# A gated recurrence: k normalised in channels by rows like q, two products on ScalarE, single buffers

## The reference, cut to what matters

```python
q = silu(causal_dwconv(xn @ Wq, qconv_w, qconv_b))      # 4 taps
k = silu(causal_dwconv(xn @ Wk, kconv_w, kconv_b))
v = xn @ Wv
beta = sigmoid(xn @ Wb + bb)                            # one per token and head
q = layernorm(q per head, qn_w, qn_b); k = layernorm(k per head, kn_w, kn_b)
def step(S, inp):                                       # over the tokens
    S = (1.0 - b) * S + b * (v_t[..., :, None] * k_t[..., None, :])
    o_t = einsum('bhvk,bhk->bhv', S, q_t)
o = o * silu(xn @ Wg); s = o @ Wo
```

## Time and profile before

| engine | busy us | share of the span |
|---|---|---|
| TensorE (PE) | 2504.8 | 95% |
| VectorE (DVE) | 1813.8 | 69% |
| ScalarE (ACT) | 1083.8 | 41% |
| GpSimd (POOL) | 848.1 | 32% |

### The profile page before, as it was taken

One profiled execution on the slowest core, in us unless ns is written; L12 is line 12 of the kernel. 1 busy time (PEld: TensorE's weight loads), 2 busy tenths in 40 slices (PEclk: granted clock), 3 DMA queues, 4 the chain that ended last, 5 costly groups with the idle time before them and its releaser, 6 DMA issues. The chain is left out here.

```text
span 2627.0 us, 43782 instructions
## 1 busy us (share of the span) xinstructions
PE 2504.8 (95%) x15296; PEld 2215.4 (84%) x15296; DVE 1813.8 (69%) x3332; ACT 1083.8 (41%) x1513; POOL 848.1 (32%) x442
## 2 busy tenths in 40 slices
PE   4889999999999999999999999997899998999997
PEld 4778888889999989999989999996788887888886
DVE  5589999988988888889888989887421222433232
ACT  5454455444545444444444444443433323322221
POOL 1245545434343434343434343444100000211220
PEclk8989999999999999999999999998999999999998
DMA  7555555654445464444465444543561101431320
GB/s 272 171 177 170 192 186 176 211 192 161 160 153 168 160 224 160 165 163 152 160 215 179 155 162 158 171 154 105 164 224 49 64 32 64 135 138 49 112 87 25
DMA packets 232134, 395.10 MB, mean 150 GB/s; under 512 B 58358, under 2 KB 159990, under 8 KB 219130
## 3 DMA queue, kind: packets, MB, share of 16 engines
q1 hardware_dynamic: 125946, 192.21, 22.4%
q10 hardware_dynamic: 97408, 176.71, 19.9%
q0 software_dynamic: 8704, 25.19, 3.1%
HBM read 304.88 MB, written 97.55 MB: 153 GB/s over the span
## 5 line engine op out<-in xcount | busy, mean ns | idle before, releaser
L1005 DVE SCALAR_TENSOR_TENSOR xn_rows<-ps_proj,conv,xn_rows 128x1021 f32<-128x1021 f32 x381 | 486.6, 1277 | 11.6 <-ACT xn_rows L895 2.5
L1208 PE MATMUL ps_proj<-xt_hi,w_hi 128*128 128x512 f32 x1008 | 413.0, 410 | 14.5 <-DVE xn_rows L1005 8.1
L1210 PE MATMUL ps_proj<-xt_hi,w_lo 128*128 128x512 f32 x1008 | 397.9, 395 | 0.0
L1209 PE MATMUL ps_proj<-xt_lo,w_hi 128*128 128x512 f32 x1008 | 396.6, 393 | 0.0
L786 POOL TENSOR_TENSOR rc_k_state<-rc_tok_k,k_norm_rows 128x1024 f32<-128x1024 f32 x64 | 153.7, 2402 | 587.4 <-DVE rc_q_silu L1052 502.6
L1230 PE MATMUL ps_proj<-wv_hi,xt_hi 128*128 128x256 f32 x1024 | 294.9, 288 | 0.6 <-PEq L75 0.6
L1231 PE MATMUL ps_proj<-wv_lo,xt_hi 128*128 128x256 f32 x1024 | 289.5, 283 | 0.0
L1232 PE MATMUL ps_proj<-wv_hi,xt_lo 128*128 128x256 f32 x1024 | 289.4, 283 | 0.0
L1208 PEld LDWEIGHTS ps_proj<-xt_hi,w_hi 128*128 128x128 f32 x1008 | 191.1, 190 | 53.5 <-issue 11.7
L819 POOL TENSOR_TENSOR rc_rstd_shift<-rc_small,rc_minus_half 128x16 f32<-128x16 f32 x64 | 187.2, 2924 | 124.8 <-DVE rc_small L1036 124.8
L1210 PEld LDWEIGHTS ps_proj<-xt_hi,w_lo 128*128 128x128 f32 x1008 | 190.3, 189 | 42.7
(11 more groups left out here) (181 smaller groups left out, 5766.8 us busy)
## 6 DMA issues: line engine op xcount, KB each, us to landing
rc_q_rows<-scratch_q_rows ACTq DMA_DIRECT2D x64, 1024.0 KB, 4.9
rc_decay_all<-scratch_decay ACTq DMA_DIRECT2D x64, 512.0 KB, 3.7
rc_cum_all<-scratch_cum ACTq DMA_DIRECT2D x64, 512.0 KB, 3.9
scratch_o<-rc_o_sb ACTq DMA_DIRECT2D x64, 512.0 KB, 4.4
w_hi<-scratch_w_split SPq DMA_DIRECT2D x48, 512.0 KB, 4.1
w_lo<-scratch_w_split SPq DMA_DIRECT2D x48, 512.0 KB, 5.2
wv_hi<-scratch_wv_split SPq DMA_DIRECT2D x24, 512.0 KB, 3.9
wv_lo<-scratch_wv_split SPq DMA_DIRECT2D x24, 512.0 KB, 4.8
```

The costliest lines, as they stand in the source:

```text
L1005: nc.vector.scalar_tensor_tensor(out=act_cm[j][:, back:], in0=projected[:, 0:L - back], scalar=conv[par][:, j, t:t + 1], in1=act_cm[j][:, ...
L1208: nc.tensor.matmul(out, hi, xt_hi[:, k, cols], start=k == 0, stop=False)
L1209: nc.tensor.matmul(out, hi, xt_lo[:, k, cols], start=False, stop=False)
L1210: last = nc.tensor.matmul(out, lo, xt_hi[:, k, cols], start=False, stop=k == KC - 1)
```

## The change

For k the turn back to channels goes away. The rows of k's 1/sigma and shift are turned, stored and loaded like q's (32 rows instead of 16 in one store; two loads), VectorE scales k in channels (`k_silu` has two buffers and `k_rows` is new), and ScalarE applies weight and bias one step later, for D. The product of v and beta becomes eight ScalarE operations of 128 columns behind the silu of q, and the decay of k's state eight ScalarE operations behind the tap of k. `decay_all`, `cum_all`, `k_cm` and `o_sb` have one buffer instead of two, with waits for the head before instead of the one before that. The loads of the sums move behind the decayed state in ScalarE's list. In the first stage one semaphore takes the place of two. The buffers of `ps_work` are now chosen by the parity of the step too.

```diff
-        k_cm = two("k_cm", [P, L])
+        k_cm = sb("k_cm", [P, L])
-        decay_all = two("decay_all", [P, L])
-        cum_all = two("cum_all", [P, L])
+        decay_all = sb("decay_all", [P, L])
+        cum_all = sb("cum_all", [P, L])
-        o_sb = two("o_sb", [P, NC, P])
+        o_sb = sb("o_sb", [P, NC, P])
...
             def load_decay(par, i, pair):
-                after_step(act, "dmat_done", i - 2)
+                after_step(act, "dmat_done", i - 1)
...
             def load_cum(par, i, pair):
-                after_step(act, "states_done", i - 2, NC - 1)
-                after_step(act, "q_cum_done", i - 2)
+                after_step(act, "states_done", i - 1, NC - 1)
+                after_step(act, "q_cum_done", i - 1)
...
+                def ready_k():
+                    after_step(act, "k_scaled", D_.i, 2)
+                    after_step(act, "scores_mm", D_.i - 1)
+                    nc.scalar.activation(k_cm[:], k_silu[D_.par][:], ACT.Identity,
+                                         bias=norm[:, 1, 1:2], scale=norm[:, 1, 0:1]).then_inc(S["k_ready"], 1)
...
+                def load_rows(j, X):
+                    after_step(act, "rows_stored", X.i, 16)
+                    after_step(act, "qk"[j] + "_scaled", X.i - 1, 2)
+                    parts = row(scratch["rows"], X.i)[2 * L * j:2 * L * (j + 1)]
+                    act.dma_start((q_rows, k_rows)[j][:].rearrange("p k t -> p (k t)"), parts.partition_broadcast(P)
+                                  ).then_inc(S["qk"[j] + "_rows_loaded"], 16)
+
+                def decayed_state():
+                    after_step(act, "k_tokens_done", C_.i)
+                    after_step(act, "dmat_done", C_.i)
+                    for c in range(NC):
+                        last = nc.scalar.activation(k_state[C_.par][:, c], k_state[C_.par][:, c], ACT.Copy,
+                                                    scale=dmat[C_.par][:, c, P - 1:P])
+                    last.then_inc(S["k_state_done"], 1)
...
+                def gate_values():
+                    after_step(act, "v_projected", B_.i)
+                    after_step(act, "outputs_mm", 2 * B_.pair - 3)
+                    stand(act, keep["carrier_sp"])
+                    first = B_.par * VC
+                    for c in range(VC):
+                        for h in range(2):
+                            columns = slice((2 * c + h) * P, (2 * c + h + 1) * P)
+                            last = nc.scalar.activation(
+                                v_beta[B_.pair_par][:, first + c, h], ps_proj[:, B_.par, columns], ACT.Identity,
+                                scale=keep["beta_steps"][:, first + c, bass.ds(B_.pair * 2 + h, 1)])
+                    last.then_inc(S["v_beta_done"], 1)
...
                 if B_.live:
                     silu(0)
+                    gate_values()
+                if D_.live:
+                    ready_k()
+                if B_.live:
                     silu(1)
...
                 if C_.live:
-                    ready(0, "q_scaled", 2, q_silu[C_.par][:], "q_ready", q_cm[C_.par])
+                    ready_q()
+                    load_rows(1, C_)
...
-                if C_.live:
-                    ready(1, "k_back", 1, work(KB), "k_ready", k_cm[C_.par])
-                    load_cum(C_.par, C_.i, C_.pair)
                 if B_.live:
                     tokens()
                 if A_.live:
                     tap(1)
+                if C_.live:
+                    decayed_state()
+                    load_cum(C_.par, C_.i, C_.pair)
                 if B_.live:
                     store_rows()
...
-                    load_rows()
+                    load_rows(0, B_)
...
 # VectorE
+            def scale(j, C_):
+                n = "qk"[j]
+                values, rows = (q_silu, k_silu)[j][C_.par], (q_rows, k_rows)[j]
+                after_step(dve, n + "_rows_loaded", C_.i, 16)
+                after_step(dve, n + "_turned", C_.i)
+                nc.vector.tensor_tensor(values[:], values[:], rows[:, 0], ALU.mult).then_inc(S[n + "_scaled"], 1)
+                after_step(dve, n + "_scaled", C_.i, 2, 1)
+                nc.vector.tensor_tensor(values[:], values[:], rows[:, 1], ALU.add).then_inc(S[n + "_scaled"], 1)
...
-                if B_.live:
-                    gate_values()
                 if C_.live:
...
-                    scale_q()
+                    scale(0, C_)
...
                 if C_.live:
-                    after_step(dve, "k_tokens_done", C_.i)
-                    after_step(dve, "dmat_done", C_.i)
-                    nc.vector.tensor_tensor(k_state[C_.par][:], k_state[C_.par][:],
-                                            dmat[C_.par][:, :, P - 1:P].to_broadcast([P, NC, P]), ALU.mult
-                                            ).then_inc(S["k_state_done"], 1)
+                    scale(1, C_)
...
 # TensorE
-                if C_.live:
-                    after_step(pe, "k_normed", C_.i)
-                    if first_done(D_.i):
-                        after_step(pe, "k_ready", 0)
-                    after_step(pe, "outputs_done", D_.i - 1)
-                    turn(work(KB), lambda c: tok_k[:, c]).then_inc(S["k_back"], 1)
...
-                    nc.tensor.transpose(work(SC)[0:2 * NC, 0:P], rstd_shift[:, 0].rearrange("p k c -> p (k c)"),
-                                        ident[:]).then_inc(S["q_rows_turned"], 1)
+                    nc.tensor.transpose(work(par, SC)[0:4 * NC, 0:P], rstd_shift[:].rearrange("p j k c -> p (j k c)"),
+                                        ident[:]).then_inc(S["rows_turned"], 1)
```

More of the change, by code:

```diff
@@ L272, in statistics @@
             def statistics(n, par):
-                after(dve, S["mean_done"], n)
+                after(dve, S["stats_done"], 2 * n)
                 for c in range(NC):
@@ L599, in stage_recurrence @@
         VC = NC // 2
-        QT, KB, KT, UP, SC, OUT = range(6)
+        QT, KT, UP, SC, OUT = range(5)
         class At:
@@ L876, in step, with ready_q @@
                 A_, B_, C_, D_, nxt = (At(u, par, lag, odd) for lag in (0, LAG_B, LAG_C, LAG_D, -1))
+                past = At(u, par, LAG_D + 1, odd)
                 proj_of = lambda pos: ps_proj[:, (par + pos) % 2]
-                def ready(j, name_in, per, source, name_out, out):
-                    after_step(act, name_in, C_.i, per)
+                def ready_q():
+                    after_step(act, "q_scaled", C_.i, 2)
                     after_step(act, "scores_mm", C_.i - 2)
[L883 to L886, removed]
+                    after_step(act, "q_cum_done", C_.i - 2)
+                    nc.scalar.activation(q_cm[C_.par][:], q_silu[C_.par][:], ACT.Identity,
+                                         bias=norm[:, 0, 1:2], scale=norm[:, 0, 0:1]).then_inc(S["q_ready"], 1)
@@ L909, in store_rows @@
[L909 to L921, removed]
+                    after_step(act, "rows_turned", B_.i)
@@ new lines, in store_rows @@
+                    after_step(act, "rows_stored", B_.i - 1, 16)
+                    nc.scalar.activation(row_parts[:], work(par, SC)[0:4 * NC, 0:P], ACT.Copy
+                                         ).then_inc(S["rows_copied"], 1)
+                    after_step(act, "rows_copied", B_.i)
+                    act.dma_start(row(scratch["rows"], B_.i).rearrange("(m p) -> m p", p=P), row_parts[:]
+                                  ).then_inc(S["rows_stored"], 16)
+                def load_rows(j, X):
[4 more added lines that the diff above has]
+                                  ).then_inc(S["qk"[j] + "_rows_loaded"], 16)
@@ L1013, in statistics @@
                     after_step(dve, ("q_turned", "k_tok")[j], B_.i)
-                    tokens = (chunks(work(QT)), tok_k)[j]
+                    tokens = (chunks(work(par, QT)), tok_k)[j]
                     for c in range(NC):
@@ L1055, in gate_values @@
[L1055 to L1064, removed]
@@ L1178, in _, with work @@
         def _(pe):
-            def work(pos):
-                return ps_work[:, pos % 2]
+            def work(par, pos):
+                return ps_work[:, (par + pos) % 2]
             def turn(out, source):
@@ L1257, in step @@
                     after_step(pe, "k_silu", B_.i)
-                    after_step(pe, "stats_done", B_.i, 2, 1)
-                    turn(work(KT), lambda c: act_cm[1][:, c * P:(c + 1) * P]).then_inc(S["k_turned"], 1)
+                    if isinstance(D_.i, int) and D_.i <= 0:
+                        after_step(pe, "stats_done", B_.i - 1, 2, 1)
+                    else:
+                        after_step(pe, "outputs_done", D_.i - 1)
+                    turn(work(par, KT), lambda c: k_silu[B_.par][:, c * P:(c + 1) * P]).then_inc(S["k_turned"], 1)
                 if D_.live:
@@ L1300, in step @@
                     for c in range(NC):
-                        out = work(OUT)[:, c * P:(c + 1) * P]
+                        out = work(par, OUT)[:, c * P:(c + 1) * P]
```

(2 more changed lines are left out.)

113 lines of the change are left out of this document (51 added, 62 removed).

## The result

The changed kernel takes 2715.67 us (median of 4 runs, 2710.25 to 2718.92) against 2628.46 (2627.04 to 2629.53); ratio 1.033, 95% interval 1.0312 to 1.0348. The profiled execution took 2714.48 us, span 2712.7. Predicted were 2604 us, range 2588 to 2638: wrong in sign.

A forecast was written before the change was run, and what follows sets the result against it. TensorE's own work was taken to bound the 44 middle steps: 0.88 us saved less 0.33 mean stall gives 0.55 a step, 24 us. 2628.8 - 24.2 - 1 (last four steps) = 2603.6, so 2604 us, range 2588 to 2638.

The forecast's parts named there:

- k's decayed state on ScalarE: ScalarE after the k tap, idle for 7.09 us: eight operations, some 2.5 us (up to 3.85), costed at nothing.
- The transposes back: TensorE loses the eight transposes back of k: 0.88 us a step, 38.7 us in 44 middle steps.
- G: Price of v x beta as eight ScalarE operations behind the silu of q: 2.17 us, bounds 1.02 and 3.85.
- The stall in late steps: TensorE waits for ScalarE's v x beta before its first k projection in every other middle step: 0.65 us, mean 0.33.
- early steps: The 22 middle steps whose silu of q starts about 6.14 us after the step's opening row turn: no stall.
- The late steps of T + 7.2: Late steps whose silu starts near 7.2 us after T, the step's opening row turn; others near 6.7, mean 6.95.
- the landing of the cum load: Cum load, issued later, lands about 1.3 us into the next step beside the row store: 0.2 us, bounds 0 and 1.3.
- rival C: No stall, if the eight operations take 1.5 us or less or late steps lose their lag: 2589 us; chance 0.09.
- Rival A: ScalarE is the slower place: v x beta's eight operations take 3.20 us, 13 us slower, 2641 us; chance 0.21.
- VectorE, more DMA, the decay buffer, one output buffer: Side effects costed at nothing: VectorE's total unchanged, 1 MB more a step, decay-buffer wait already implied, store has a whole step.
- The first stretch: First 17 steps, 131.6 to 577.2 us, where GpSimd's chain sets the end: change of 0, bounds -10 and +10.

The follow-up runs named there:

- run 10: Changed kernel, loops kept, with 4 more long-met wait instructions on VectorE and 64 on ScalarE ahead of the second loop: 2599.05 us, one run.
- run 1: Changed kernel with the second loop (head pairs 8 to 29) written out on ScalarE and VectorE, other engines keeping theirs: 2592.39 us, ratio 0.9864.
- run 7: The written-out changed kernel of run 1 with the eight transposes of k done twice, the first time for nothing: 2632.71 us, one run.
- run 8: The written-out changed kernel of run 1 with v x beta as one VectorE operation again, in place of ScalarE's eight: 2595.94 us, one run.
- run 5: Kernel before the change, with 90 more long-met wait instructions on VectorE ahead of its second loop: 2659.61 us, one run.

## Why the prediction was wrong, step by step

**The step that failed** is "k's decayed state on ScalarE: eight operations ... after the k tap, where ScalarE was idle", under what was costed at nothing, and, in the same way, the eight of v x beta, which were priced in time alone: I gave each new operation a duration and a place in time and none in the program. Sixteen operations a step in place of none, four steps a round, with the waits and register work around them, made ScalarE's loop 321 instructions long, and VectorE's, which I called neutral, moved. The jumps cost 119.5 us in the middle stretch, where the step stood for 0; 114.3 of them are the reloading (1242.94 - 1128.66, run 10), the rest is about what the jumps cost with their loops in place. A trace of it was in my rows: the third silu of the earlier trace rows says "1.14 <-issue". That is the jump back of the loop of before, with everything still loaded. I read it as one more late step.

**The transposes back, 0.88 us in 44 steps, 38.7 us:** right. 1161.80 - 1123.39 = 38.4 in run 1, and 37.4 put back in run 7.

**G, the eight ScalarE operations, 2.17 us:** right. The changed kernel at the step of 665.9 us:
```profile
671.99 1.06 ACT L941 ACTIVATE rc_q_silu<-xn_rows 128x1024 f32<-128x1024 f32 x1 [0.76 <-ACT rc_o_sb L1005]
672.95 2.16 ACT L953 ACTIVATE rc_v_beta<-ps_proj,beta_steps 128x128 f32<-128x128 f32 x8
```
One lasts 380 ns by the groups (predicted 350) and starts are 0.25 apart (predicted 0.26): two small errors that nearly cancel. The estimate of 2.44 us from the Trainium skill (ScalarE: Activation LUTs, What ACT_TABLE_LOAD costs) was 0.28 too much.

**The stall in late steps, 0.65 each, 14 us:** mis-sized. In run 10, where the loops stay and only the slow jumps are gone, early steps take 25.3, late ones inside the round about 25.45 and those at the jump about 25.9: stalls of 0.15 and 0.6. The late steps of T + 7.2 were the ones at the jump, and the 0.2 us for the landing of the cum load did not show. Written out there is no jump: silu starts at T + 5.7 in early steps and at about T + 6.4 and T + 6.65 in late ones, in turn. With 0.96 + 2.16 + 0.1 behind it the first kind of late step ends below the 9.73 of TensorE's side, the second at 9.87; these last about 25.38 us, a stall of 0.1, and most of them take 25.29 in run 8, where ScalarE has no v x beta. That is a condition of rival C (the late steps lose their lag), and 2592 about its time (2589).

**Rival A** had the right sign for another reason: its eight operations at 3.20 us are not there.

**VectorE, more DMA, the decay buffer, one output buffer:** nothing, as costed, though tried only together. With the jumps out of the way VectorE has 1029.1 us in the middle (1025.8 before), and TensorE's waits there, from 585 to 1700 us, are 2.7 us for x and 2.0 for VectorE and ScalarE. Two buffers again for the output weren't tried: the memory has no room for them beside k's rows and silu buffers.

**The first stretch:** I wrote 17 steps; 131.6 to 577.2 are 16, 27.85 us each. It took 445.6 us before, 456.2 in the changed kernel, 451.3 in run 1, 454.2 in run 10. Predicted was 0, bounds 10; the changed kernel's 10.6 lie just outside. Of these, 6.0 are TensorE's wait for the next sequence's x (6.7 against 0.7), and 3.1 of run 1's 5.7 (3.8 against 0.7). TensorE's wait for VectorE's shift grew from 16.9 to 24.2 us, and to 23.8 in run 1, as the transposes' time was to go into it; the rest is not settled.

The sum, without the step that failed: 2628.8 - 38.4 + 5.7, and 2.7 less at both ends, gives 2593.4, against a profiled time of 2593.5 in run 1 (span 2591.7, and 1.8).

## What to carry to other kernels

An operation moved into a loop on another engine has a place in the program as well as a duration: count the loop's instructions on each engine before and after, and look for "issue" in front of a loop's first work, and at the packets of the instruction queue. When a changed kernel is slow in a few steps out of each round and right in the others, write the loop out before judging the change: here it was worth 1.4% and showed as 3.3% lost. Where a loop has to stay, a few empty instructions ahead of it can decide 50 us, so a count that fits today is undone by the next edit.

## What the runs showed of the hardware

A jump back costs ScalarE 1.14 us even with its loop still loaded. Where the loop has to be loaded, the first instruction comes 5.1 to 6.3 us late on ScalarE and 3.5 to 3.7 on VectorE in the changed kernel, and 2.3 to 2.5 on VectorE in run 5.

In the changed kernel a pause on another engine cost TensorE twice, once as idling and once as a lower clock behind it. Windows of the changed kernel behind its wait for the silu:
```profile
647.90:650.00 2.10, 2.10 (x9) 1.76 (x10) 0.12 (x1) 2.10 (x9) 1.97 (x1) 0.50 0.00 0
650.00:652.00 2.00, 2.00 (x7) 1.63 (x8) 1.56 (x8) 1.88 (x3) 2.00 (x2) 0.74 0.00 0
652.00:654.00 2.00, 2.00 (x11) 1.63 (x10) 0.83 (x1) 2.00 (x3) 2.00 (x2) 1.00 0.54 184
...
675.15:677.15 2.00, 2.00 (x7) 1.52 (x5) 2.00 (x4) 1.76 (x2) 0.00 (x0) 0.50 0.07 1
```
After 3.27 us of idling the clock granted is 0.50, the 1.2 GHz level, and it is full, 2.4 GHz, from 652 on. After the wait of 3.59 us the products come 0.43 apart instead of 0.23, from 673.74 to about 678, and the clock granted there is 0.50 too. In all, TensorE is busy 1163.3 us in the middle for the 7615 products that take 1117.7 in run 1, at a mean granted clock of 0.96 against 1.00: of the 119.5 us lost, 45.6 are its own slower work and 73.9 its idling.
